# Score groups for the maxima through four PSUM banks, and batches that begin with turned groups

## What is computed

```python
x = x + tanh(g_xattn[0]) * decayed_scan(layernorm(x), ctx)
x = x + tanh(g_ffn[0]) * fp4_ffn(layernorm(x))
q, k, v = rope(layernorm(x)), rope(ctx), ctx            # 16 heads of 16 columns
scores = einsum('bqhd,bkhd->bhqk', q, k) / 4 + slope[h] * (key - query)
x = x + tanh(g_xattn[1]) * softmax(scores) @ v
x = x + tanh(g_ffn[1]) * bfp_ffn(layernorm(x))
```

## Times and profile before

| | us |
|---|---|
| median of 3 runs (848.14, 848.79, 858.55) | 848.79 |
| the profiled execution | 849.06 |
| its span, first to last instruction | 847.0 |
| negated maxima of batch 0 to those of batch 15 (L941) | 366.95 to 665.59 |

### The profile page before, as it was taken

The page is one execution under the profiler, slowest core; times in us unless marked ns, Lnnn a source line. Parts: engine busy times, 40 slices in busy tenths (PEclk is TensorE's granted clock), DMA queues, the critical chain, the costliest instruction groups (busy, mean ns, idle before and its releaser), DMA issues.

```text
span 847.0 us, 16572 instructions
## 1 busy us (share of the span) xinstructions
PE 707.5 (84%) x5075; PEld 514.2 (61%) x5090; DVE 695.7 (82%) x1230; ACT 488.6 (58%) x955; POOL 431.4 (51%) x331
## 2 busy tenths in 40 slices
PE   2365999999999996889999999999999765777775
PEld 1255888888888885556555665656555433444444
DVE  6866888888888878779888889888888658888985
ACT  3343555555554432357777777777777675556553
POOL 3523665556656655444554445554444425655463
PEclk9987999999999999979999999999999897888999
DMA  8710000000000000010000000000001000000011
GB/s 272 221 43 0 1 1 1 0 0 0 0 0 1 1 2 0 1 51 2 2 3 1 1 1 1 1 1 1 1 1 51 2 1 5 34 25 25 26 38 50
DMA packets 17719, 18.35 MB, mean 22 GB/s; under 512 B 1670, under 2 KB 16912, under 8 KB 17680
## 3 DMA queue, kind: packets, MB, share of 16 engines
q1 hardware_dynamic: 17084, 17.66, 6.5%
q10 hardware_dynamic: 596, 0.20, 0.1%
HBM read 13.39 MB, written 4.19 MB: 21 GB/s over the span
## 4 chain that ended last, share of the span: by engine, by line
PE 51%; DVE 22%; issue 12%; ACT 7%; POOL 5%; DMA 1%; DVEq 1%; POOLq 0%; ACTq 0%; SPq 0%
PE ps_o L528 9%; PE a_ps_t L567 7%; PE a_ps_m L585 6%; DVE maxima L1509 5%; PE a_ps_pv L621 4%; DVE f_ps_small L1594 4%; PE ps_gu L492 4%; PE ps_gu L494 4%; PE ps_gu L493 4%; PE a_ps_s L606 3%; DVE f_hcode L1610 2%; PE a_ps_pv L629 1%; ACT stack_t L920 1%; PE f_ps_h L709 1%; ACT probs L929 1%
## 5 line engine op out<-in xcount | busy, mean ns | idle before, releaser
L1509 DVE TENSOR_REDUCE maxima<-a_ps_m 128x2 f32<-128x512 f32 x256 | 166.1, 685 | 36.5 <-PE a_ps_m L585 35.7
L929 ACT ACTIVATE probs<-a_ps_s 128x512 f32<-128x512 f32 x256 | 149.4, 602 | 43.5 <-PE a_ps_s L606 41.1
L585 PE MATMUL a_ps_m<-stack_t 64*128 64x256 f32 x512 | 109.1, 332 | 19.7 <-DVE maxima L1509 16.7
L585 PEld LDWEIGHTS a_ps_m<-stack_t 64*128 64x128 f32 x512 | 69.5, 192 | 79.3 <-DVE maxima L1509 49.9
L606 PE MATMUL a_ps_s<-stack_t 64*128 64x256 f32 x512 | 100.5, 310 | 4.6 <-ACT probs L929 3.7
L1152 POOL TENSOR_TENSOR stack<-roped,stack 128x512 f32<-128x512 f32 x32 | 42.7, 1335 | 116.2 <-DVE stack L1499 114.7
L528 PE MATMUL ps_o<-w2t,hqt 128*128 128x256 f32 (+1 forms) x384 | 99.6, 394 | 1.2 <-ACT hqt L857 0.7
L492 PE MATMUL ps_gu<-w1h,yth 128*128 128x352 f32 x256 | 86.8, 339 | 4.7 <-DVE h L1322 4.7
L621 PE MATMUL a_ps_pv<-probs,v_aug 128*32 128x256 f32 x1024 | 83.5, 398 | 2.9 <-ACT probs L929 2.7
L920 ACT CAST stack_t<-a_ps_t 128x512 fp32r<-128x512 f32 x128 | 71.0, 588 | 23.5 <-PE a_ps_t L567 22.2
L567 PE MATMUL a_ps_t<-idf,stack 128*128 128x128 f32 x512 | 76.0, 289 | 8.7 <-POOL stack L1152 4.3
(11 more groups left out here) (178 smaller groups left out, 1608.9 us busy)
## 6 DMA issues: line engine op xcount, KB each, us to landing
xres<-in_x SPq DMA_DIRECT2D x16, 256.0 KB, 3.2
ctx<-in_ctx SPq DMA_DIRECT2D x16, 256.0 KB, 4.1
out_x<-f_y SPq DMA_DIRECT2D x16, 256.0 KB, 2.1
w1a_raw<-in_w_gate_up SPq DMA_DIRECT2D x1, 1024.0 KB, 5.9
w_raw<-in_w_fc SPq DMA_DIRECT2D x1, 1024.0 KB, 5.4
w_raw<-in_w_proj SPq DMA_DIRECT2D x1, 1024.0 KB, 4.8
w_raw<-in_w_down SPq DMA_DIRECT2D x1, 704.0 KB, 9.9
stack_t<-neg_max_t SPq DMA_DIRECT2D x32, 8.0 KB
```

The costliest lines, as they stand in the source:

```text
L585: ins = nc.tensor.matmul(a_ps_m[:, half, n, :], a_stack_t[b.par][rows, 0, pair, c * P:(c + 1) * P], a_stack_t[b.par][rows, 1, pair, :], st ...
L929: nc.scalar.activation(a_probs[:, u % 8], a_ps_s[:, u % 2], ACT.Exp).then_inc(a_exp, 1)
L1509: nc.vector.tensor_reduce(a_maxima[:, b.par, c, 4 * quad + half:4 * quad + half + 3:2], a_ps_m[:, half], X, ALU.max).then_inc(a_v_max, 1)
```

## The change

- `max_bank`: the 16 score groups for the maxima now go through four banks. Groups 4, 5, 8, 9, 12 and 13 use the two banks of `a_ps_t`, the other ten those of `a_ps_m`.
- Groups 4 and 5 wait for ScalarE's copies of the turned groups 6 and 7, whose banks they take, in place of a wait for VectorE. Groups 2 and 3 still wait for the reduction two before; from group 6 on each waits for the reduction four before.
- The turned groups 0 and 1 of the next batch wait for the reductions 12 and 13, in place of copies 6 and 7.
- `at_turn_max` moves from the end of a body to behind turned group 1 of the next body, `at_max_out` to behind the copy of turned group 0. In the last body, which turns nothing, both stand first.
- No instruction is added or removed.

```diff
+LAST_IN_TURN_BANKS = 6
...
+        def max_bank(m):
+            pair, half = m // 2, m % 2
+            if pair >= 2 and pair % 2 == 0:
+                return a_ps_t[:, half, :].rearrange("p (a t) -> p a t", t=T)
+            return a_ps_m[:, half]
+        def group_in_same_max_bank(m):
+            return m - 4 if m >= 6 else m - 2
...
                 elif b.shifted(-1):
-                    pe.wait_ge(a_t, b.shifted(-1).count(TG, TG + g - 1))
+                    pe.wait_ge(a_v_max, b.shifted(-1).count(MU, 2 * LAST_IN_TURN_BANKS + g + 1))
...
-                if m >= 2:
-                    pe.wait_ge(a_v_max, b.count(MU, m - 1))
+                if m in (4, 5):
+                    pe.wait_ge(a_t, b.count(TG, TG + m - 5))
+                elif m >= 2:
+                    pe.wait_ge(a_v_max, b.count(MU, group_in_same_max_bank(m) + 1))
...
@@ TensorE, at_body @@
                 if not nxt:
+                    at_turn_max(b)
...
                         at_turn(nxt, g)
+                        if g == 1:
+                            at_turn_max(b)
...
                 at_times_v(b, PG - 1)
-                if nxt:
-                    at_turn_max(nxt)
...
@@ ScalarE, at_body @@
                 if nxt:
-                    for g in range(6):
+                    at_turned(nxt, 0)
+                    at_max_out(b)
+                    for g in range(1, 6):
                         at_turned(nxt, g)
                 else:
+                    at_max_out(b)
...
                 at_pv_out(b, 3)
-                if nxt:
-                    at_max_out(nxt)
```

More of the change, by code:

```diff
@@ L584, in at_scores_for_max @@
                     pair = 2 * quad + n
-                    ins = nc.tensor.matmul(a_ps_m[:, half, n, :], a_stack_t[b.par][rows, 0, pair, c * P:(c + 1) * P],
+                    ins = nc.tensor.matmul(max_bank(m)[:, n, :], a_stack_t[b.par][rows, 0, pair, c * P:(c + 1) * P],
                                            a_stack_t[b.par][rows, 1, pair, :], start=True, stop=True)
@@ L770, in _ @@
                 at_scores_for_max(first, m)
-            at_turn_max(first)
             pe.wait_ge(v_out, B)
@@ L1047, in _ @@
                 l0_hidden_out(last, g)
-            at_max_out(first)
             over_batches(act, at_body)
@@ L1508, in at_row_max @@
                     dve.wait_ge(a_t_mt, b.shifted(-2).count(1, 1))
-                nc.vector.tensor_reduce(a_maxima[:, b.par, c, 4 * quad + half:4 * quad + half + 3:2], a_ps_m[:, half], X,
+                nc.vector.tensor_reduce(a_maxima[:, b.par, c, 4 * quad + half:4 * quad + half + 3:2], max_bank(m), X,
                                         ALU.max).then_inc(a_v_max, 1)
```

## The result

The changed kernel takes **829.39 us** (median of 4 runs, 828.24 to 830.41), against 849.38 us of the kernel before (4 runs on the same chip). The ratio is 0.9749, 95% interval 0.9717 to 0.9782: faster by 2.5%. Forecast were 830 us with a range of 824 to 839, so time and range held. The inner working held only in part: some of its terms were off, in opposite directions.

A forecast was written before the change was run, and what follows sets the result against it. No single bound: TensorE and VectorE wait for each other. 13 batches at 1.12 us each (14.6) plus edges 4.3 give 18.9 us off 849.06, so 830 us, range 824 to 839.

The forecast's parts named there:

- End gap: VectorE's gap before reduction 13 of a batch, 0.39 and 0.31 us; claimed to go, 0.35 us per batch.
- Middle gap: VectorE's gap before reduction 4 of a batch, 0.55 us; claimed to stay.
- rival 3: All of VectorE's gaps go, the one before reduction 4 too: a further 13 x 0.45, about 824 us; chance 0.10.
- Front gap: VectorE's gap before reduction 0 of a batch, 1.01 and 0.68 us; claimed to fall by 1.54 us per pair.
- rival 2: Last times-v group doesn't come earlier, because exponentials hold it; turned maxima come late, about 842 us; chance 0.08.
- First scores by the row's landing: Batch front: the row of maxima becomes the last wait, first scores 3.04 us after the negation's start, 3.68 after the last reduction.
- Edges: Outside the 13 steady batches: 1.0 us before body 0, 1.0 in body 0, 2.3 in body 14, together 4.3.
- Clock rival: TensorE's clock falls in every batch to a mean of 0.80, so the kernel gets slower, about 867 us; chance 0.05.

The follow-up runs named there:

- the best version: Against the kernel before: the changed kernel with four banks in strict turn and the turned maxima behind one turned group in place of two; 824.35 us, ratio 0.9688.

## Why the prediction was right, and where it wasn't

- **End gap: right.** Four banks take it away (0.35 us a batch), and do so alone.
- **Middle gap: right.** It stayed at 0.55 us. That four banks in strict turn shorten it to 0.34 us and win 3.5 us in the batches was rival 3's direction, for another kernel.
- **Front gap: mis-sized.** The step that failed is "In the change TensorE has finished its last times-v group earlier ... I take 0.9 of the 1.29 us". It ended 0.1 us ahead of the last reduction and not 0.9, and the turned groups and turned maxima came that much later; the prices behind them (0.4 to the negation, 3.04 to the first scores, 2.65 to reduction 0) were right. The front gave 0.34 us a batch in place of 0.77. The turned maxima at 0.82 us behind the last reduction are the very sign that the prediction had named for rival 2, and rival 2's mechanism is there in part. But its reason, that exponentials hold the group, fell with the moved copy of v, and ScalarE was waiting for scores itself. What holds it is TensorE's own row of work: between the first group and the last times-v group it waits for no reduction, more work of its own makes the batch longer (0.23 of 0.27 us), and with more work for VectorE the group does end 0.77 us ahead. I let TensorE run ahead by the distance of the banks without asking whether its 17.9 us of work left it room in a batch of 18.5. The windows showed a number of this size before.
- **Missed in the other direction:** 0.36 us a batch of waits too short to be printed as gaps went with the banks. They were in the rows: 9.14 us from reduction 4 to the statistics, of which I looked only at the gap of 0.39. The two errors, -0.43 and +0.36, nearly cancel: 1.05 for 1.12 in the pair of batches that the prediction had before it. The 1.10 over all 13 holds the disturbed batch of the kernel before, 1.1 us in all. The time was right in part by luck.
- **First scores by the row's landing: right** in its price, 3.04 to 3.11 us, and there was next to no slack (though the scores came 4.3 to 4.4 us behind the last reduction and not 3.7, for the front gap's reason): TensorE stood 1.77 of the 1.83 us by which the row was made late, and a negation 0.17 us earlier moved the first scores by as much in every second batch.
- **Edges: too small.** 6.3 us against 4.3, from one execution of each kernel. Such an edge varies: with the same code ahead of it the first negation came at 365.24, 365.70 and 366.14 in three executions, and body 14 had a mean clock of 0.85 before and 0.92 after. Against the gain stand 1.9 us that the profiled execution lost behind the last negation. There TensorE's clock was at its lower level for at least 8 us, where the execution before had the full clock in the same place (1.00 in each of three windows of 4 us from 668.6):

```profile
652.00:656.00 4.00, 3.99 (x26) 1.91 (x24) 2.47 (x10) 3.60 (x9) 1.16 (x3) 0.50 0.01 2
656.00:660.00 4.00, 4.00 (x34) 2.53 (x36) 2.75 (x9) 3.08 (x5) 0.98 (x2) 0.50 0.00 0
```

  The other three executions of the changed kernel have a mean clock of 0.95 to 0.955, where the profiled one has 0.938, and take 0.6 to 2.2 us less. What decides it was not tried. These 1.9 us and the 2.0 at the edges are a second pair of errors that cancel.
- **Clock rival: right to exclude here, real elsewhere.** The steady batches kept 1.00. The Trainium skill, "TensorE: Matmul & The Clock Gate", section "A second HAM failure mode: psum-queue depth-cycling", reports a clock that swings with frequent short idles while cycling through banks. Four banks with gaps of up to 0.26 us didn't show it in the steady batches of this trace; behind a wait of 1.8 us a batch the clock did fall.

What stays open is why TensorE's busy time shrank with the waits, and what lowers the clock in single batches and edges: in the best version's execution body 0 had a mean clock of 0.89 and took 20.29 us, in the changed kernel's 0.97 and 19.19.

## What to carry to other kernels

When two engines exchange buffers and neither is fully busy, read the idle time of the busier one first, as a rough ceiling of what more buffers can gain (here 1.3 to 1.5 us of a batch, of which 1.0 came, and 1.4 in the best version). It is no strict one: the best version still had 0.46 us idle, since the busy time itself fell by 0.4. Only then read the gaps of the other engine, since a gap of the less busy engine may simply come back as slack. Measure a stretch of back-to-back operations from its first start to its last end and divide by their number: waits too short to be printed are only seen so. And when two changes come together, try each alone, since here one was worth nothing until the other was there.

## What the runs showed of the hardware

Behind a wait of TensorE for the late row, of 1.77 us in the batch shown, in otherwise dense work, the granted clock fell in twelve of 13 batches, in that one to a mean of 0.68 over 4 us; in the thirteenth the wait was 1.35 us and the clock stayed at 1.00, and behind one of 1.63 us in body 0 the mean of the batch was 0.99. Waits of 0.70 us were followed by a fall in one batch of the kernel before and not in the other twelve. A transfer queued behind two others on the same queue let the first scores start 1.83 us later, 0.9 us for each. Reductions of 128x512 out of PSUM that find their data ready follow each other every 0.60 us although each is recorded as 0.68 us long.
